# Expert 1's turning put in expert 2's bank, and the head and the first turn put in another order

## What is computed

```python
xn = _layernorm(x)
q, k, v = xn @ q_w, xn @ k_w, xn @ v_w                  # 32 columns each
scores = (q @ k.T) * decay ** max(diff - 1, 0) * (diff > 0)
att = (scores @ v) @ o_w.T * out_scale

logits = xn @ router_w + router_b + load_balancer
rw, sel = top_k(logits, 2); rw = softmax(rw)
e0 = silu(xn @ sw_w1) * (xn @ sw_w3) @ sw_w2
e1 = gelu(((xn @ me_eq_w + ..) @ me_wv + ..) @ me_wo + .. @ me_c1w + ..) @ me_c2w + me_c2b
syn = xn @ ce_syn_w + ce_syn_b
h2 = _layer_norm(syn + (syn @ ce_wv + ce_bv) @ ce_wo + ce_bo)
h2 = _layer_norm(h2 + relu(h2 @ ce_f1w + ..) @ ce_f2w + ..)
e2 = h2 @ ce_gen_w + ce_gen_b
e3 = gelu(xn @ ml_w1 + ml_b1) @ ml_w2 + ml_b2
out = x + att + sum of rw * (the chosen two of e0..e3)
```

## Time and profile before

| | us |
|---|---|
| median of 3 runs | 442.94 |
| the runs | 442.23 to 443.46 |
| the profiled execution's own time | 438.38 |
| its span, first to last instruction | 436.6 |
| TensorE busy | 423.8 (97%) |
| VectorE busy | 382.2 (88%) |
| ScalarE busy | 338.6 (78%) |
| GpSimd busy | 330.4 (76%) |

### The profile page before, as it was taken

One profiled execution on the slowest core, in us unless ns is written; L12 is line 12 of the kernel. 1 busy time (PEld: TensorE's weight loads), 2 busy tenths in 40 slices (PEclk: granted clock), 3 DMA queues, 4 the chain that ended last, 5 costly groups with the idle time before them and its releaser, 6 DMA issues.

```text
span 436.6 us, 9605 instructions
## 1 busy us (share of the span) xinstructions
PE 423.8 (97%) x2610; PEld 355.0 (81%) x2610; DVE 382.2 (88%) x1132; ACT 338.6 (78%) x788; POOL 330.4 (76%) x464
## 2 busy tenths in 40 slices
PE   4989999999999999999999999999999999999996
PEld 4768888887887888788788888888787888878886
DVE  4775999898988989898898998989899898989897
ACT  4977878699786978978798786878978787894860
POOL 3798497795859868696896859779685987857494
PEclk9999999999999999999999999999999999999999
DMA  7522525535353452534435262553535345252321
GB/s 259 48 50 98 94 53 133 111 100 100 92 107 85 120 116 87 109 90 103 95 109 100 92 129 49 137 103 100 98 90 113 79 126 114 97 99 74 72 50 49
DMA packets 154307, 42.91 MB, mean 98 GB/s; under 512 B 128976, under 2 KB 146096, under 8 KB 154288
## 3 DMA queue, kind: packets, MB, share of 16 engines
q1 hardware_dynamic: 154000, 42.67, 42.3%
q10 hardware_dynamic: 288, 0.01, 0.0%
HBM read 22.53 MB, written 19.92 MB: 97 GB/s over the span
## 4 chain that ended last, share of the span: by engine, by line
PE 69%; POOL 8%; DVE 6%; issue 5%; POOLq 4%; DMA 3%; SPq 2%; ACT 2%; DVEq 0%
PE S L1308 11%; PE EX L1229 10%; PE S L1310 10%; PE S L1309 10%; POOL hid3l L563 3%; PE S L1407 2%; PE S L1403 2%; PE S L1402 2%; SPq L407 2%; PE EX L1262 2%; PE S L1323 1%; PE S L1322 1%; PE S L1321 1%; PE TR L1350 1%; PE ATT L1334 1%
## 5 line engine op out<-in xcount | busy, mean ns | idle before, releaser
L563 POOL TENSOR_TENSOR hid3l<-hid,hid3h 128x512 fp32r<-128x512 f32 x64 | 81.0, 1299 | 63.7 <-ACT hid3h L724 63.7
L1308 PE MATMUL S<-xh,WH 128*128 128x512 f32 x224 | 91.8, 410 | 0.0
L1310 PE MATMUL S<-xh,WL 128*128 128x512 f32 x224 | 88.5, 395 | 0.0
L1309 PE MATMUL S<-xl,WH 128*128 128x512 f32 x224 | 88.2, 394 | 0.0
L1229 PEld LDWEIGHTS EX<-scaled,hid 128*128 128x128 f32 x480 | 55.3, 192 | 3.5 <-DVE OUT L945 2.8
L1229 PE MATMUL EX<-scaled,hid 128*128 128x128 f32 x480 | 56.6, 276 | 0.3 <-DVE OUT L945 0.3
L1310 PEld LDWEIGHTS S<-xh,WL 128*128 128x128 f32 x224 | 42.1, 188 | 10.1
L1019 DVE TENSOR_TENSOR hid<-gate,S 128x512 f32<-128x512 f32 x64 | 44.0, 688 | 6.0 <-DVE half L1096 2.5
L1308 PEld LDWEIGHTS S<-xh,WH 128*128 128x128 f32 x224 | 42.1, 188 | 8.4
L1309 PEld LDWEIGHTS S<-xl,WH 128*128 128x128 f32 x224 | 42.4, 189 | 7.9
L1011 DVE SCALAR_TENSOR_TENSOR gate<-th,S 128x512 f32<-128x512 f32 x64 | 43.3, 677 | 0.8 <-ACT th L690 0.2
(11 more groups left out here) (218 smaller groups left out, 1132.1 us busy)
## 6 DMA issues: line engine op xcount, KB each, us to landing
X<-x SPq DMA_DIRECT2D x16, 256.0 KB, 3.5
turning<-xn SPq DMA_DIRECT2D x15, 256.0 KB, 2.1
xb<-turning SPq DMA_DIRECT2D x60, 64.0 KB, 2.6
turning<-e3T SPq DMA_DIRECT2D x15, 256.0 KB, 2.0
turning<-u SPq DMA_DIRECT2D x15, 256.0 KB, 2.3
ub<-turning SPq DMA_DIRECT2D x60, 64.0 KB, 2.6
e3b<-turning SPq DMA_DIRECT2D x60, 64.0 KB, 2.7
turning<-e1T SPq DMA_DIRECT2D x15, 256.0 KB, 2.5
```

The source lines that it names most:

```text
L563: pool.tensor_tensor(hid3l[:, j, :], hid[3][:, j, :], hid3h[:, j, :], ALU.subtract) \
L1308: pe.matmul(bank[:, :], wh, hi, start=True, stop=False)
L1309: pe.matmul(bank[:, :], wh, lo, start=False, stop=False)
L1310: pe.matmul(bank[:, :], wl, hi, start=False, stop=True).then_inc(unit_ready, 1)
```

## The change

At the seam of the turns, expert 1 is transposed into `EX1`, and its sum goes behind `u` on VectorE; the first `x_low` goes ahead of `u`. TensorE's expert 0 waits for `e1_laid` (ScalarE's eviction) instead of the sum. In the head, the moments of x come after two decay steps; the low parts of the folds come behind `xn`; seven products of the identity are added ahead of everything, the five ahead of the transposes are taken out, and those behind become six; ScalarE casts the first weights before it takes the folds, and lays `back` two blocks at a time. In the first turn, `backh` and two small scalings go behind `h2`; `backl` moves from VectorE to GpSimd, behind `norm_x(next)`; `fold_first` goes behind the attention, `fold_second` behind `b3`, `fold_last` behind `e3`; `n1` is turned ahead of `b1`, and the masked scores go between the two halves of `silu(1)`.

```diff
@@ GpSimd, turn
                     norm_x(g.next())
+                    pool.wait_ge(back_high, 1)
+                    pool.tensor_tensor(backl[:, :], back[:, :], backh[:, :], ALU.subtract).then_inc(back_low, 1)
@@ ScalarE, head
             act.copy(TH[:, P:LOGW], w("router")).then_inc(setup_act, 1)
+            high_weights(0)
             act.wait_ge(setup_mm, MM.index("ce") + 1)
...
-            high_weights(0)
...
             act.wait_ge(pool_const, POOL_CONSTS)
             act.wait_ge(setup_act, 1)
-            for t in range(NT):
-                act.copy(back[t * C:(t + 1) * C, t * P:(t + 1) * P], oT[:, :]).then_inc(back_laid, 1)
+            lay_back(range(0, 2))
             take_x(Group(0, 0))
-            act.wait_ge(back_laid, NT)
-            act.copy(backh[:, :], back[:, :]).then_inc(back_high, 1)
             high_weights(1)
-            act.wait_ge(w_loaded[LOAD_OF["gen_w"]], DMA_INC)
-            act.mul(gen_s[:, :], w("gen_w"), vec("n2g")).then_inc(setup_act, 1)
-            act.copy(bcast[:, 1, :], vec("n2b").broadcast_to([P, P])).then_inc(setup_act, 1)
+            lay_back(range(2, NT))
@@ ScalarE, turn
                 if first:
+                    act.wait_ge(back_laid, NT)
+                    act.copy(backh[:, :], back[:, :]).then_inc(back_high, 1)
+                    scale_gen()
                     high3(0)
-                    high3(1)
-                    high3(2)
-                    high3(3)
...
                 act.copy(foundh[:, :], ATT[:, 0, :]).then_inc(found_taken, 1)
-                if not first:
-                    high3(2)
-                    high3(3)
+                if first:
+                    high3(1)
+                high3(2)
+                high3(3)
@@ VectorE, head: ahead of the low parts of the folds
+            dve.wait_ge(setup_act, 2)
+            dve.tensor_tensor(TL[:, P:LOGW], w("router"), TH[:, P:LOGW], ALU.subtract)
+            dve.wait_ge(first_root, 1)
+            for t in range(NT):
+                dve.tensor_scalar(xn[:, t, :], X[0][:, t, :], negmean["x"][:, t:t + 1], rstd["x"][:, t:t + 1],
+                                  ALU.add, ALU.mult).then_inc(x_normed, 1)
@@ VectorE, expert2, sum_expert1, sum_expert3
-                dve.wait_ge(ex_taken[1], g.count(1, 1))
+                dve.wait_ge(ex_taken[0], g.count(1, 1))
...
-                dve.wait_ge(ex_taken[0], g.count(1, 1))
-                dve.transpose(EX[EX_BANK[1]][:, :, :].rearrange("p t n -> p (t n)"),
+                dve.wait_ge(ex_taken[2], g.count(1, 1))
+                dve.transpose(EX[EX_BANK[2]][:, :, :].rearrange("p t n -> p (t n)"),
...
-                dve.wait_ge(ex_taken[2], g.count(1, 1))
+                dve.wait_ge(ex_taken[1], g.count(1, 1))
@@ VectorE, turn
                 times(2)
                 if first:
+                    fold_second()
+                silu(3)
+                if first:
                     fold_last()
-                silu(3)
-                if not first:
-                    sum_expert1(g.prev())
                 if not last:
                     turn_next(g)
                 if not first and not last:
                     expert2(g.prev())
+                if not last:
+                    x_low(g.next())
                 f2, free = unit("f2")
                 dve.scalar_tensor_tensor(out=u[:, :], in0=f2[:, :], scalar=vec("f2b"), in1=h2[:, :],
                                          op0=ALU.add, op1=ALU.add).then_inc(free, 1)
-                if not last:
-                    x_low(g.next())
...
                 if not first:
+                    sum_expert1(g.prev())
                     sum_expert3(g.prev())
@@ TensorE
+            pe.wait_ge(pool_const, IDENT_CONSTS)
+            for _ in range(IDLE_FIRST):
+                pe.matmul(ATT[:, 0, :], ident[:, :], ident[:, :], start=True, stop=True)
...
-            idle_products(IDLE_BEFORE, P // 2)
...
             def expert0(g):
-                wait(pe, ex_taken[1], g.count(1, 0))
+                wait(pe, e1_laid, g.count(1, 0))
...
             def expert3(g):
-                pe.wait_ge(ex_taken[1], g.prev().count(1, 1))
+                pe.wait_ge(e1_laid, g.prev().count(1, 1))
...
@@ constants
-DECAY_BEFORE_X = 8
-IDLE_BEFORE = 5
-IDLE_BEHIND = 3
+DECAY_BEFORE_X = 2
+IDLE_FIRST = 7
+IDLE_BEHIND = 6
+IDENT_CONSTS = 6
```

More of the change, by code:

```diff
@@ L668, in _, with lay_back, scale_gen @@
             act.copy(TH[:, 0:P], prod("ce")).then_inc(fold_high, 1)
[L669 removed]
+            def lay_back(tiles):
+                for t in tiles:
+                    act.copy(back[t * C:(t + 1) * C, t * P:(t + 1) * P], oT[:, :]).then_inc(back_laid, 1)
+            def scale_gen():
+                act.wait_ge(w_loaded[LOAD_OF["gen_w"]], DMA_INC)
+                act.mul(gen_s[:, :], w("gen_w"), vec("n2g")).then_inc(setup_act, 1)
+                act.copy(bcast[:, 1, :], vec("n2b").broadcast_to([P, P])).then_inc(setup_act, 1)
             act.wait_ge(pool_const, POOL_CONSTS)
             act.wait_ge(setup_act, 1)
[L672 to L673 removed]
+            lay_back(range(0, 2))
             take_x(Group(0, 0))
[L675 to L676 removed]
             high_weights(1)
[L678 to L680 removed]
+            lay_back(range(2, NT))
             def turn(g, first, last):
@@ L856, in _ @@
             took(dve.tensor_tensor(TL[:, 0:P], prod("ce"), TH[:, 0:P], ALU.subtract))
[L857 to L862, removed]
             product("ce_b")
@@ L871, in _ @@
             x_low(Group(0, 0))
-            dve.wait_ge(back_high, 1)
-            dve.tensor_tensor(backl[:, :], back[:, :], backh[:, :], ALU.subtract).then_inc(back_low, 1)
             dve.wait_ge(vec_loaded, DMA_INC)
@@ L944, in sum_expert1 @@
                 for t in range(NT):
-                    ins = dve.scalar_tensor_tensor(out=OUT[g.par][:, t, :], in0=EX[EX_BANK[1]][:, t, :],
+                    ins = dve.scalar_tensor_tensor(out=OUT[g.par][:, t, :], in0=EX[EX_BANK[2]][:, t, :],
                                                    scalar=coef[g.par][:, t, 1:2], in1=OUT[g.par][:, t, :],
@@ L1066, in turn @@
                     .then_inc(qd_ready, 1)
-                masked_scores()
+                if not first:
+                    masked_scores()
                 dve.wait_ge(h2_high, g.count(1, 1))
                 dve.tensor_tensor(h2l[:, :], h2[:, :], h2h[:, :], ALU.subtract).then_inc(h2_low, 1)
+                swish(1)
                 if first:
-                    fold_second()
-                silu(1)
+                    masked_scores()
+                times(1)
                 if not first:
@@ L1075, in turn @@
                 found_rest(g)
+                if first:
+                    fold_first()
                 if not first:
@@ L1346, in turn, with turn_n1 @@
                 ins.then_inc(unit_ready, 1)
[L1347 to L1351, removed]
+                def turn_n1():
+                    for t in range(NT):
+                        pe.wait_ge(c_normed, g.count(NT, t + 1))
+                        ins = pe.transpose(TR[:, t * P:(t + 1) * P], n1[:, t, :], ident[:, :])
+                    ins.then_inc(c_turned, 1)
+                three("a1", SPLIT["w1"] + P, h, l)
+                if first:
+                    turn_n1()
+                three("b1", SPLIT["w3"] + P, h, l)
+                if not first:
+                    turn_n1()
                 pe.wait_ge(qk_split, g.count(1, 1))
@@ L1375, in attend @@
                     ins.then_inc(found_ready, 1)
-                if first:
-                    fold_second()
-                else:
+                if not first:
                     attend()
@@ L1385, in turn @@
                     attend()
-                if first:
-                    fold_last()
-                if first:
+                    fold_first()
                     pe.wait_ge(back_low, 1)
@@ L1408, in turn @@
                 ins.then_inc(unit_ready, 1)
+                if first:
+                    fold_last()
                 bank = fill("f2")
```

6 lines of the change are left out of this document (1 added, 5 removed).

## The result

| | before | changed |
|---|---|---|
| median, same job | 442.59 us (4 runs, 441.22 to 443.46) | 452.64 us (4 runs, 452.52 to 452.87) |
| the profiled execution's own time | 438.38 | 452.52 |
| its span | 436.6 | 450.7 |

The kernel became slower: ratio 1.0231, 95% interval 1.0203 to 1.0258. The forecast was 453.0 (447.5 to 459.0). The two spans differ by 14.1 us, the medians by 10.1; the second is smaller because the median of before stands 4.2 above its profiled execution, and the changed kernel's only 0.1. One execution of the kernel before, on the chip of experiments 1 and 2, took 2371.59 us; it is left out of every ratio, and nothing here explains it.

What follows compares the result with a forecast made beforehand. TensorE was taken to bound each turn, busy for all of its 25.72 us. Terms -1.8 + 13.3 - 1.0 + 1.6 = +12.1 on 438.4 gave 450.5; with the median's excess 455.0; middle 453.0 us, range 447.5 to 459.0.

Steps and rivals of the forecast that it cites:

- The seam: Between turns: VectorE idles 1.0 us for `coef_r`, `pl` starts 0.95 us late, 14 times: +13.3 us (11.9 to 15.4).
- The slack of 0.1 and the refilling: At `a0` in each seam: TensorE's stall is 0.1 us less by slack, plus about as much for refilling.
- The stalls taken away: Steady turns: TensorE's expert 0 no longer waits for expert 1's sum on VectorE, -1.8 us.
- x's cast: ScalarE's `xh`, needed by `x_low` at the seam: taken at nothing; other bound +9 us.
- The rival that it would not: x's load comes no sooner, so VectorE also waits for `xh`: +9 us, 459 to 464; chance 0.10.
- The head and the first turn: Start of the kernel: earlier moments of x, limited by `backl` on GpSimd; -1.0 us (+0.5 to -2.0).
- The tail: Last turn: VectorE idles for `u`, then expert 1's work comes behind the moments of u; +1.6 us (1.0 to 2.0).
- The base: Whole kernel: whether the median's 4.6 us above the profiled execution stays after the change; middle taken, 453.0 us.
- two cases, 450.5 and 455.0: Timed result: 450.5 us if the excess is waits for expert 1's blocks and vanishes, 455.0 if spread evenly.
- The case that it is waits for late transfers: Excess of the median is longer waits for expert 1's blocks, 0.33 us per seam, vanishing with the edit: 450.5 us.

Runs made afterwards that it cites:

- Experiment 1: Kernel before with only the seam's edits: 453.9 us, ratio 1.033; changed kernel with the seam of before: 438.79 us, ratio 0.9967.
- experiment 2: Expert 1 transposed into the attention's bank, VectorE's old order: on the kernel before 440.3 us, ratio 1.0008; with the changed head and first turn 438.88, 0.9972.
- experiment 3: Changed kernel with `u` ahead of expert 2: 447.39 us; with GpSimd's power for `u` left out: 445.92; kernel before without that power: 437.96.
- experiment 4: Changed kernel with expert 3 in the attention's bank, summed ahead of expert 2: 438.26 us, ratio 0.9923; also `backl` back on VectorE: 437.48, 0.9935.
- experiment 5: Changed kernel without the seven identity products, one timed and profiled run: span 450.7 us, own time 452.49.
- the seam alone: Kernel before with the seam's edits only (expert 1's bank, VectorE's order, TensorE's wait), old head and first turn: 453.9 us, ratio 1.033.
- the kernel with the gap filled: Changed kernel with expert 3 transposed into the attention's bank and summed between `turn_next` and expert 2: 438.26 us, ratio 0.9923.

## Why the prediction was right

**The seam** is the step that carries it, and it held as put: `pl` 1.04 us late against 0.95, in 11 of 14 seams (more in three, see the cast), by the wait for `coef_r`, without the delay growing or shrinking. Two small terms make the difference: expert 2's four sums with their wait took 1.05 and not 1.00, and expert 1's sum with the wait on its own semaphore 1.23 and not 1.16. The slack of 0.1 and the refilling behind the wait cancelled, as forecast. Experiment 1 shows that the seam is the whole loss, experiments 3 and 4 that the idle time in it is the cause: with 0.66 of work in it, 0.6 goes; with enough, the usual turn is back at 25.7.

**The stalls taken away** (-1.8) did go, but the step that named them was half right. They were put down to TensorE's wait for the sum; experiment 2 shows that without this wait the time is the same (ratio 1.0008), with `pl` late in five turns behind the same blocks and one turn long through `u`'s.

**x's cast**, taken at nothing: nearly so. Of its 4 waits (1.4 us) two lie in the head and the first turn and two at seams, where the turns behind them last 27.12 and 27.24, 0.8 us too long in sum. A third turn, of 27.16, is long for another reason: expert 3's transpose ahead of it starts 0.46 late. Its blocks can't be the cause, for they had been asked for between 48.0 and 50.7, and no such transfer took over 3.2 us. What it was stays open; the kernel of experiment 5 has the same gap at the same place. The three, VectorE in order of time:

```profile
66.22 0.73 DVE L980 STREAM_TRANSPOSE EX<-e3b 128x512 f32<-128x512 f32 x1 [0.46 <-DVE OUT L952]
...
116.86 0.69 DVE L878 TENSOR_TENSOR xl<-TR,xh 128x512 fp32r<-128x512 f32 x1 [0.23 <-ACT xh L646]
...
170.87 0.69 DVE L878 TENSOR_TENSOR xl<-TR,xh 128x512 fp32r<-128x512 f32 x1 [0.36 <-ACT xh L646]
```

The load of x did come sooner against the turn (its wait 16.9 and not 26.1), as argued. The rival that it would not was a small part of the truth.

**The head and the first turn**: -1.24 for -1.0, with `x_low` at 10.98 for 10.9, `backh`'s product at 25.96 for 26.15, and TensorE waiting 1.14 for `backl`. The -1.24 is that of two executions, and the one of before starts its second turn late for its kind: at 41.16, where the three other kernels with the old head and first turn start it at 40.43 to 41.04. The six with the new ones and `backl` on GpSimd (experiment 5 left out) start it at 39.84 to 40.10, so the gain is 0.9 on average, nearer to the forecast.

**The tail**: 35.91 from the last turn's start, 33.55 before. 1.04 of the 2.36 are that turn's own stall, 1.3 the tail; forecast 1.6 (its terms, -0.26 + 1.93, give 1.7).

In the sum over the profiled executions: -1.2 + 13.0 (14 distances, 25.85 to 26.78 in the mean) + 2.4 = 14.1, where the terms of the prediction give 12.1. Of the 2.0 missing, 1.2 are the seam's 0.09 x 13, 1.2 the three turns of 27.12 to 27.24, 0.1 the last turn's stall, and the head and the tail give 0.5 back.

**The base** was open in the prediction, and the middle between two cases, 450.5 and 455.0, was taken: 452.75, written as 453.0, so 2.5 above what the terms give. The changed kernel's median stands 0.1 above its profiled execution. So 453.0 came near 452.64 by luck in part, for two errors cancel: 2.0 too little for the change, 2.4 too much for the base. What the excess of before is remains open; in the experiments its median stood some 2 to 3 us above the profiled execution, not 4.6. The case that it is waits for late transfers fits the changed kernel's narrow range in that job (0.35 us) and the turns of 26.9 to 27.2 of the kernels with a tight seam, in which blocks of `u` or of expert 1, or x's cast, come late. Against it, the seam alone ranged from 452.48 to 455.05 on another chip, though its seam is as loose. No timed run has a trace, so this was not settled.

## What to carry to other kernels

Where an engine in program order has a full stretch of work between two gates, here some 6 us of VectorE's ahead of `pl`, the order inside it decides: an instruction that waits for another engine must have work ahead of it that waits for nothing, and whoever moves such work away pays the idle time, once per turn. A bank or a semaphore that is named in the waits is not yet the cause; ask what comes late if it is gone, for the same lateness may surface at the next gate. Take the sum of such a stretch by the distances from start to start in the trace, add each new wait, and compare with the gate of the bounding engine.

## What the runs showed of the hardware

The granted clock reads 1.00 (the level of 2.4 GHz) from the first microsecond in the kernel before and in the changed one, yet in the head of the kernel before a product of 128 columns (two records) takes 0.43 us from start to start, and 0.22 in the changed one at 7.24 to 7.90, behind 3.4 us of identity products and the first folds. Without the identity products it is 0.43 again until 9.5 us. The granted clock of the profile doesn't show this. The row of the kernel before that stands beside those at 7.46 and 8.24:

```profile
8.19 0.64 PE L1167 MATMUL S<-ident,W 128*128 128x128 f32 x2
```

A power is dear on GpSimd: 1.02 us for 128x4 elements, against 0.20 for an addition of the same size. Its length, once a turn, makes most of the gap: without it the wait for `coef_r` falls from 17.0 to 5.4 us. GpSimd of the kernel before, in order of time:

```profile
216.38 0.20 POOL L621 TENSOR_TENSOR veps_u<-mv_u,eps 128x4 f32<-128x4 f32 x1
216.73 1.02 POOL L623 TENSOR_TENSOR rstd_u<-veps_u,nhalf 128x4 f32<-128x4 f32 x1
```

Transfers of one shape land at uneven times in one execution. In the kernel with the gap filled, the 60 loads of expert 1's blocks, 64 KB each, took 2.3 to 3.7 us from issue to landing:

```profile
DMA to landing us min/median/max: 2.3/3.0/3.7
```

SP's waits there for its store of `xn` (sum, times, longest) were 1.2 us in the mean and 3.1 at the longest; part of that spread may be when SP came to wait. A seam without slack pays for each late one, as the turns of experiments 2 and 4 show:

```profile
SPq L407 <- DMA turning<-xn: 17.7, 15, 3.1
```
